# Keeping the residual stream transposed through both FFNs of a macaron block, with LayerNorm applied by GpSimd

## The chip, the core and the metric

The kernel runs on one core of one Trainium2 chip. The metric is device microseconds of one execution. A core has five engines with queues of their own: TensorE (PE), VectorE (DVE), ScalarE (ACT), GpSimd (POOL) and SyncE (SP), which here only issues DMAs.

## What is computed

A batch of 8 sequences of 1024 tokens with 128 features goes through FFN, attention and the same FFN again, in float32. Each stage is preceded by a LayerNorm without weights.

```python
x = x + 0.5 * ffn(layernorm(x))
x = x + attn(layernorm(x))
x = x + 0.5 * ffn(layernorm(x))

def ffn(x):                                    # T = 8192 tokens, D = 128
    scores = sigmoid(x @ gate_w.T)             # 16 experts
    _, idx = top_k(scores + gate_b, 4)
    w = scores[idx] / sum(scores[idx]) * 2.5   # comb: (T, 16), 4 entries a token
    for e in range(16):                        # all experts, INTER = 64
        gate, up = split(x @ w13[e].T)
        y += comb[:, e] * ((silu(gate) * up) @ w2[e].T)
    gate, up = split(x @ w13_s.T)
    return y + (silu(gate) * up) @ w2_s.T
```

## The kernel before

The 8192 tokens are 16 tiles of 512. `X` in SBUF holds the whole residual stream with tokens on the partitions. All matmuls of the FFN want features on the partitions, so a tile is transposed on the way in and its result on the way back. One 512-column product is three matmuls of split operands (`mm3`: high by high, high by low, low by high; `_h` and `_l` in the names), all of which stand in line L1318.

A tile T of an FFN is nine units j = 0 to 8 (eight pairs of experts and the shared expert). For each unit PE makes the gate and the up product (3 + 3 matmuls of 512 columns), ACT applies silu to the gate (L586), DVE multiplies by the routing weights (`ffn_weighted`, L933) and by up (`ffn_h`, L943), ACT rounds the result to `h_h` (`ffn_h_hi`, L551), POOL subtracts to get `h_l` (`low_half`, L412), and PE adds the down product three units later (LAG = 3), so that the downs of units 6 to 8 of a tile stand in units 0 to 2 of the next one. The two banks of gate, of up and of Y are used in turn.

Around these units lie, per tile:

- LayerNorm of tile T+2: DVE takes the statistics (`ffn_stats`, `ffn_mv`, `ffn_var`), POOL makes `rstd` and `neg_shift` (L416 to L421), ACT applies them to four blocks of 128 tokens (`ffn_xn`, L558).
- PE turns `xn` of tile T+1 with four 128x128 transposes at the start of the tile (`ffn_xnT`, L1402). ACT copies the bank to `xh`, DVE subtracts to get `xl` (L837).
- PE makes the router's logits of tile T+1 in unit 1; DVE works out the routing weights `comb` in some ten small instructions; PE turns `comb` in unit 5 (`ffn_combT`, L1416), ACT copies it, SP writes it to DRAM (L336) and reads it back broadcast over 64 partitions a row into `comb_b`, the memory of `qkT` (L341, ten DMAs).
- ACT copies the finished Y of tile T-1 to `yT`, PE turns it with four transposes in unit 4 (`ffn_y`, L1423), DVE adds it to `X` (`residual`, L987). In the second FFN SP then stores the tile.

Eight transposes a tile are thus of the residual stream. The loops over tiles take two tiles an iteration on every engine. Attention runs over 8 sequences in 8 steps each; its prologue is woven into the last two tiles of the first FFN, and the opening of the second FFN (`ffn_prep`) into the last sequence.

The order on each engine is written by hand and fixed; engines meet only through semaphores that count up. The edit touches these waits, among others:

```python
def ffn_combT(T):
    pe.wait_ge(route_step, ROUTE * (T + 1))
def ffn_down(T, q, j):
    pe.wait_ge(h_lo_done, UNITS * T + j + 1)
```

Of the kernel before, what the change touches and what calls it, by code (L numbers as in the profile page):

```python
# [14 lines left out]
P = 128  # L15
B, M, D = 8, 1024, 128
INTER, NEXP, TOPK = 64, 16, 4
ROUTE_SCALE = 2.5
EPS = 1e-5
# [11 lines left out]
PT_CHUNKS = 12  # L31

# [10 lines left out]
END_BANK = 4, 7  # L43
# [44 lines left out]
def macaron(nc, x, w13T, w2T, wqkvT, gwT, gate_b, ident_d, mask_d, cos_d, sin_d, comb_d, out):  # L88
    x_v = x.rearrange("b (n p) d -> p (b n) d", p=P)
    out_v = out.rearrange("b (n p) d -> p (b n) d", p=P)  # L90

    with ExitStack() as ctx:
# [9 lines left out]
        X = sb("X", [P, (B + 1) * QB, D])  # L102
        ident = sb("ident", [P, P])
# [48 lines left out]
        combT = [sb(f"combT{q}", [NEXP * NB, P]) for q in range(2)]  # L152
# [10 lines left out]
        v = [stage[:, v_at + p * M:v_at + (p + 1) * M].rearrange("p (n d) -> p n d", d=D) for p in range(2)]  # L163
        rope_c = [sb(f"rope_c{p}", [P, TILE]) for p in range(ROPE_BUFS)]
# [18 lines left out]
        yT = probT[0][:, NB:2 * NB, :].rearrange("p a c -> p (a c)")  # L183
# [13 lines left out]
        x_loaded = [sem(f"x_loaded{n}") for n in range(3)]  # L197
# [25 lines left out]
        neg_shift_done = sem("neg_shift_done")  # L223
        xn_done = sem("xn_done")
# [10 lines left out]
        comb_loaded = [sem(f"comb_loaded{n}") for n in range(len(COMB_PAIRS))]  # L235
# [8 lines left out]
        yT_done = sem("yT_done")  # L244
        yT_half = sem("yT_half")
        y_ready = sem("y_ready")
        y_half = sem("y_half")
        x_done = sem("x_done")
        stored = sem("stored")
# [41 lines left out]
        def end_blocks(a):  # L291

            at = NB * (TILES - 1) + NB // 2 * a
            return slice(at, at + NB // 2)
# [8 lines left out]
        def ln_count(T):  # L303

            return T + 1

# [4 lines left out]
        def _(sp):  # L311
# [10 lines left out]
            load(X[:, NB:2 * NB, :], x_v[:, NB:2 * NB, :], x_loaded[1])  # L322
            load(w13_f[:, early[2], :], w13T[:, early[2], :], w13_loaded[2])
            load(w2_f, w2T, w2_loaded)
            load(X[:, 2 * NB:3 * NB, :], x_v[:, 2 * NB:3 * NB, :], x_loaded[2])
# [5 lines left out]
            def comb_rows(T, q, first=0):  # L331
# [6 lines left out]
                src = comb_d[q].rearrange("(j a) t -> a j t", a=2)  # L338
                for g, (j0, j1) in enumerate(COMB_PAIRS):
                    for a in range(2 if j0 >= first else 0):  # L340
                        sp.dma_start(comb_b[q][a * INTER:(a + 1) * INTER, j0:j1, :],  # L341
                                     src[a:a + 1, j0:j1, :].to_broadcast([INTER, j1 - j0, TILE])
                                     ).then_inc(comb_loaded[g], 16)

            def store(t):
                sp.wait_ge(x_done, TILES + 1 + t)
                sp.dma_start(out_v[:, tile_blocks(t), :], X[:, tile_blocks(t), :]).then_inc(stored, 16)

            def ffn(base, stores):
                comb_rows(base, 0, 0 if stores else SPREAD)  # L350
                if stores:
                    sp.wait_ge(scores_ready, B * QB)
                else:
                    load(wqkv_f, wqkvT, attn_loaded)
                    load(mask[:], mask_d, attn_loaded)
                    load_x(3, 1)
                comb_rows(base + 1, 1)
                if not stores:
                    load_x(4, 0)
                    load(cos[:], cos_d, rope_loaded)  # L360
                    load(sin[:], sin_d, rope_loaded)
                with sp.Fori(0, TILES // 2 - (1 if stores else 3)) as k:
                    for q in range(2):
                        comb_rows(base + 2 * k + 2 + q, q)
                        if stores:
                            store(2 * k + q)
                        else:
# [1395 lines left out]
```

## Time and profile before

| | before |
|---|---|
| median of 3 runs | 861.89 us (861.54 to 862.0) |
| the profiled execution, its time | 863.0 us |
| its span | 861.2 us |
| granted TensorE clock | 0.998 |
| PE busy | 844.4 us, 98% |
| DVE busy | 694.2 us, 81% |
| ACT busy | 591.2 us, 69% |
| POOL busy | 557.6 us, 65% |
| DMA queue q1 | 88.58 MB, 41.3% of 16 engines |

The two FFNs take the stretches from 0 to about 340 us and from about 541 us to the end, attention the stretch between them. Busy shares are means over these. Ends of matmuls are modelled, so a busy PE is not a PE at its peak: the distance between the starts of two matmuls tells what one costs.

### The profile page before, as it was taken

How to read it: one execution, taken by the hardware profiler on the slowest of the kernel's cores; microseconds unless marked ns; L12 is line 12 of the kernel's file. 1: busy time of each engine (PE TensorE's matmuls, PEld its weight loads, DVE VectorE, ACT ScalarE, POOL GpSimd, SP SyncE). 2: the span in 40 equal slices, each digit the busy share in tenths (PEclk: the TensorE clock that was granted, in tenths of full speed). 3: DMA queues.
4: the chain of work that ended last, by engine and by line, in shares of the span. 5: the costliest groups of instructions: out<-in, count | busy, mean ns of one | idle time of the engine just before them, and what ended most of it. 6: DMA issues, size and time to landing. Idle time of an engine off the chain costs nothing.

```text
span 861.2 us, 18145 instructions
## 1 busy us (share of the span) xinstructions
PE 844.4 (98%) x4506; PEld 709.0 (82%) x4506; DVE 694.2 (81%) x2125; ACT 591.2 (69%) x1215; POOL 557.6 (65%) x519
## 2 busy tenths in 40 slices
PE   8999999999999999999999999999999999999998
PEld 7788888888888876889999998788888888888886
DVE  6888888888888887777776667788888888888885
ACT  5566666666666687777778866766666666666664
POOL 6666666666666678866767762466666666666664
PEclk9999999999999999999999999999999999999999
DMA  3684444455555341222111220445545444444553
GB/s 123 185 233 113 111 111 113 114 126 131 133 122 136 101 114 36 50 51 46 38 40 25 48 49 1 111 124 129 134 124 136 111 111 111 112 112 125 127 134 82
DMA packets 63494, 89.01 MB, mean 103 GB/s; under 512 B 7520, under 2 KB 26208, under 8 KB 63200
## 3 DMA queue, kind: packets, MB, share of 16 engines
q1 hardware_dynamic: 63456, 88.58, 41.3%
q8 instruction: 14, 0.23, 0.1%
q14 instruction: 24, 0.20, 0.1%
HBM read 74.92 MB, written 5.24 MB: 93 GB/s over the span
## 4 chain that ended last, share of the span: by engine, by line
PE 52%; ACT 4%; issue 2%; DVE 2%; POOL 1%; ACTq 0%; DVEq 0%; POOLq 0%
PE bank L1318 47%; PE bank L1628 3%; PE bank L1402 1%; PE bank L1423 1%; ACT prob L740 1%; ACT probT L551 1%; ACT xn L612 1%; ACT qkT L551 1%; ACT xh L551 0%; ACT xn L558 0%; POOL qkT L412 0%; DVE prob L933 0%; DVE X L1214 0%; DVE probT L943 0%; PE bank L1416 0%
## 5 line engine op out<-in xcount | busy, mean ns | idle before, releaser
L412 POOL TENSOR_TENSOR h_l<-probT,h_h 128x512 fp32r<-128x512 f32 x254 | 328.9, 1296 | 202.8 <-ACT h_h L551 202.7
L551 ACT ACTIVATE h_h<-probT 128x512 fp32r<-128x512 f32 (+1 forms) x286 | 179.5, 628 | 72.6 <-DVE probT L943 70.0
L1318 PE MATMUL bank<-xh,w_h 128*128 128x512 f32 x544 | 223.4, 411 | 2.0 <-DVE prob L933 1.9
L586 ACT ACTIVATE bank<-bank 128x512 f32<-128x512 f32 x252 | 146.2, 580 | 103.0 <-PE bank L1318 98.6
L1318 PE MATMUL bank<-xh,w_l 128*128 128x512 f32 x544 | 214.9, 395 | 0.0
L933 DVE TENSOR_TENSOR prob<-bank,qkT 128x512 f32<-128x512 f32 x252 | 173.5, 689 | 50.6 <-ACT bank L586 37.7
L1318 PE MATMUL bank<-xl,w_h 128*128 128x512 f32 x544 | 213.2, 392 | 0.0
L943 DVE TENSOR_TENSOR probT<-prob,bank 128x512 f32<-128x512 f32 x255 | 173.8, 681 | 12.7 <-DVE biased L874 5.0
L1318 PEld LDWEIGHTS bank<-xh,w_h 128*128 128x128 f32 x544 | 102.7, 189 | 23.9 <-DVE prob L933 2.7
L1318 PEld LDWEIGHTS bank<-xh,w_l 128*128 128x128 f32 x544 | 102.5, 188 | 23.9
L1318 PEld LDWEIGHTS bank<-xl,w_h 128*128 128x128 f32 x544 | 102.9, 189 | 19.5
L1318 PE MATMUL bank<-h_h,w_h 128*128 128x512 f32 x288 | 117.7, 409 | 1.0 <-POOL h_l L412 1.0
L1318 PE MATMUL bank<-h_h,w_l 128*128 128x512 f32 x288 | 114.3, 397 | 0.2 <-ACT h_h L551 0.2
L1318 PE MATMUL bank<-h_l,w_h 128*128 128x512 f32 x256 | 101.6, 397 | 0.0
L551 ACT ACTIVATE probT<-bank 128x512 f32<-128x512 f32 (+2 forms) x129 | 63.8, 510 | 39.5 <-PE bank L1628 37.8
L1318 PE MATMUL bank<-stage,probT 128*128 128x128 f32 x576 | 76.8, 279 | 4.4 <-DVE X L1214 2.0
L1318 PEld LDWEIGHTS bank<-stage,probT 128*128 128x128 f32 x576 | 71.1, 192 | 10.0 <-issue 4.7
L558 ACT ACTIVATE xn<-X,neg_shift,rstd 128x128 f32 (+1 forms) x128 | 61.2, 485 | 9.3 <-POOL neg_shift L421 9.3
L1318 PE MATMUL bank<-qkT 128*128 128x512 f32 (+3 forms) x288 | 66.5, 358 | 0.5 <-POOL qkT L412 0.5
L1318 PEld LDWEIGHTS bank<-h_h,w_h 128*128 128x128 f32 x288 | 54.3, 189 | 15.2 <-POOL h_l L412 2.1
L1318 PEld LDWEIGHTS bank<-h_h,w_l 128*128 128x128 f32 x288 | 54.5, 189 | 11.4 <-ACT h_h L551 0.6
L502 POOL TENSOR_TENSOR rope_s<-stage,sin 128x512 f32<-128x512 f32 x32 | 41.1, 1284 | 27.0 <-DMA stage<-stage 24.8
(117 smaller groups left out, 1332.4 us busy)
## 6 DMA issues: line engine op xcount, KB each, us to landing
qkT<-comb_rows SPq DMA_DIRECT2D x190, 256.0 KB, 5.2
qkT<-comb_rows SPq DMA_DIRECT2D x124, 128.0 KB, 2.9
stage<-stage SPq DMA_DIRECT2D x64, 128.0 KB, 2.4
X<-in_x SPq DMA_DIRECT2D x16, 256.0 KB, 6.2
out_x<-X SPq DMA_DIRECT2D x15, 256.0 KB, 5.8
comb_rows<-combT SPq DMA_DIRECT2D x32, 32.0 KB, 1.8
cos<-in_cos SPq DMA_DIRECT2D x1, 1024.0 KB, 8.3
sin<-in_sin SPq DMA_DIRECT2D x1, 1024.0 KB, 10.7
```

Of the source, the lines that this page charges most:

```text
L412: nc.gpsimd.tensor_tensor(lo, f, hi.bitcast(F32), ALU.subtract).then_inc(done, 1)
L502: nc.gpsimd.tensor_tensor(rope_s[s][:], qk_x[s], sin[:, w, t], ALU.mult).then_inc(rope_s_done, 1)
L551: return nc.scalar.activation(dst, src, ACT.Copy)
L558: ins = nc.scalar.activation(xn[:, n, :], X[:, bass.ds(NB * Tx + n, 1), :].rearrange("p a d -> p (a d)"), ACT.Identity, bias=neg_shift[:, ...
L586: nc.scalar.activation(bank[:, G_BANK[g], :], bank[:, G_BANK[g], :], ACT.Silu).then_inc(silu_done, 1)
L612: ins = nc.scalar.activation(xn[:, n, :], xb, ACT.Identity, bias=shift[:, n:n + 1], scale=root[:, n:n + 1])
L740: nc.scalar.activation(prob[s][:, 0:w], bank[:, 2 * s:2 * s + 2, :].rearrange("p a c -> p (a c)")[:, 0:w], ACT.Exp, bias=negmax[s][:], sca ...
L933: nc.vector.tensor_tensor(weighted[j % 2], bank[:, G_BANK[(q + j) % 2], :], comb_b[q][:, j, :], ALU.mult).then_inc(weighted_done, 1)
L943: nc.vector.tensor_tensor(h_place(T, q, j), weighted[j % 2], bank[:, u, :], ALU.mult).then_inc(h_done, 1)
L1318: return nc.tensor.matmul(dst, lhsT, rhs, start=start, stop=stop)
L1402: ins = nc.tensor.transpose(bank[:, T_BANK, n * P:(n + 1) * P], xn[:, n, :], ident[:])
L1628: ins = nc.tensor.transpose(bank[:, probT_bank(i, c, last), a * P:(a + 1) * P], prob[s][:, k0:k0 + P], ident[:])
```

## The change

The FFNs keep the residual stream of a tile with features on the partitions, in a ring `xT` of four buffers of 512 columns (in the free part of `stage`), beside `X`.

- First FFN: x is loaded a second time, from an array that the host has transposed (`load_xT`, 256 KB a tile). The residual is added to `xT` straight from the Y bank (`residual`). PE turns the result with four transposes (`ffn_y`, now in unit 6), ACT copies them to `X` for attention (`ffn_X`).
- Second FFN: PE turns `X` of tile T+2 at the start of tile T (`ffn_xT`), ACT copies the bank to `xT`; the residual is added there, and the tile is stored to a transposed output, which the host turns back. The last tile is done in two halves.
- LayerNorm from tile 2 of each FFN on: POOL writes -mean and rstd of tile T+3 into two more columns a block of `comb` (`ffn_rows`), which travel with the routing weights through `ffn_combT` and DRAM. SP reads the two rows back, broadcast to all partitions (`rows`, one DMA of 512 KB a tile). POOL computes `xc = xT + rows[0]`, `xs = xc * rows[1]` and, after ACT has copied `xs` to `xh`, `xl = xs - xh`.
- Gone are the four ACT instructions of `ffn_xn`, DVE's `ffn_xl`, the copy `ffn_yT` and PE's `ffn_xnT` for these tiles. Tiles 0 and 1 of each FFN take the former way.
- Statistics of X are taken a tile earlier (T+3 in tile T). All loops take four tiles an iteration, and PE's code of the second FFN is written out tile by tile but for its attention part.

```diff
@@ SP
+            def load_xT(T, r):
+                sp.wait_ge(y_ready, T - RING + 1)
+                sp.dma_start(xT[r], x_t[:, bass.ds(TILE * T, TILE)]).then_inc(xT_moved[r], 16)
...
+                if ahead:
+                    wait(sp, xs_done, scaled_count(T + 1, base))
+                    sp.dma_start(rows[:], comb_d[q, NEXP:NEXP + 2, :].rearrange("(a e) t -> a e t", a=1
+                                                                                ).to_broadcast([P, 2, TILE])
+                                 ).then_inc(rows_loaded, 16)
...
+                        store(4 * k + TILES + c, c)
+                        comb_rows(4 * k + TILES + 2 + c, c % 2, 0, TILES)
@@ POOL
+            def ffn_rows(T, q):
+                pool.wait_ge(var_done, ln_count(T))
+                wait(pool, combT_ready, T - 2)
+                nc.gpsimd.tensor_tensor(comb[:, NEXP + 1, :], var_eps[:, at], neg_half[:, at], ALU.pow).then_inc(rstd_done, 1)
+                nc.gpsimd.tensor_tensor(comb[:, NEXP, :], mv[:, at, 0], neg_one[:, at], ALU.mult).then_inc(neg_mean_done, 1)
+            def ffn_center(T, base, turn, c):
+                n = scaled_count(T, base)
+                pool.wait_ge(rows_loaded, 16 * n)
...
+                nc.gpsimd.tensor_tensor(xc, xT[c], rows[:, 0, :], ALU.add).then_inc(xc_done, 1)
+            def ffn_scale(T, base):
...
+                nc.gpsimd.tensor_tensor(xs, xc, rows[:, 1, :], ALU.mult).then_inc(xs_done, 1)
+            def ffn_xl(T, q):
+                pool.wait_ge(xh_done, T + 1)
+                low_half(xl[q][:], xs, xh[q][:], xl_done)
...
+                    if j == PAIRS - 1 and ahead:
+                        ffn_xl(T + 2, q)
                     pool.wait_ge(h_hi_done, UNITS * T + j + 1)
...
-                    elif j == 2 and not last:
-                        ffn_rstd(T + 2)
+                    elif j == 2 and (t is None or t + 3 < TILES):
+                        ffn_rows(T + 3, 1 - q)
+                    if j == 3 and ahead:
+                        ffn_center(T + 2, base, turn + (c + 2) // RING, (c + 2) % RING)
+                    elif j == 5 and ahead:
+                        ffn_scale(T + 2, base)
@@ ACT
+            def ffn_xh(T, q, base):
+                act.wait_ge(gate_ready, UNITS * (T - 1))
+                act.wait_ge(xs_done, scaled_count(T, base))
+                copy(xh[q][:], xs).then_inc(xh_done, 1)
...
-                    if j == 0 and not last and not start:
-                        ffn_xh(T + 1, 1 - q)
...
+                    if j == UNITS - 1 and ahead:
+                        ffn_xh(T + 2, q, base)
...
-                    if j == LAG and not first:
-                        ffn_yT(T - 1, 1 - q)
...
-                    elif 0 <= at < NB and not last:
-                        ffn_xn(T + 2, Tx + 2, at)
@@ DVE
+            def residual(T, c, parts=1):
+                dve.wait_ge(down_done, UNITS * (T + 1))
...
+                    nc.vector.scalar_tensor_tensor(xT[c][:, cols], bank[:, Y_BANK[c % 2], cols], 0.5, xT[c][:, cols],
+                                                   ALU.mult, ALU.add).then_inc(xr_done, 1)
...
-                ffn_xl(N, 1 - q)
...
+                    if j == NB and not first:
+                        residual(T - 1, back)
...
@@ DVE, opening
                 ln_apply(NB, 0, xn_done)
+                dve.wait_ge(x_loaded[1], 16)
+                ffn_stats(1, 1, 1)
+                ffn_stats_wait(1)
+                ffn_mv(1, 1)
+                ffn_var(1, 1)
                 ffn_xl(0, 0)
-                dve.wait_ge(x_loaded[1], 16)
-                for n in range(NB):
-                    ffn_stats(1, 1, n)
-                ffn_stats_wait(1)
+                dve.wait_ge(x_loaded[2], 16)
+                ffn_stats(2, 2, 0)
+                ffn_stats_wait(2)
@@ PE
-            def ffn_combT(T):
+            def ffn_combT(T, ahead=True):
                 pe.wait_ge(route_step, ROUTE * (T + 1))
+                if ahead:
+                    pe.wait_ge(rstd_done, ln_count(T + 2))
+                    pe.wait_ge(neg_mean_done, ln_count(T + 2))
...
-            def ffn_tile(T, q, first, last, first_batch=None):
-                if not last:
+                if first:
                     ffn_xnT(T + 1)
+                if base and (t is None or t + 2 < TILES):
+                    ffn_xT(T + 2, T + 2 - base)
...
-                    if j == 4 and not first:
+                    if base:
+                        if first and j in (2, 4):
+                            ffn_xT(T + j // 2 - 1, j // 2 - 1)
+                    elif j == 6 and not first:
...
-                        ffn_y(T - 1)
+                        ffn_y(T - 1, (c - 1) % RING)
```

How the order moves on the engines. First PE, at the head of the tile loop of the first FFN, before: the branch row opens the loop, L1402 is the transposes of `xn`, then come the gate and the up product of unit 0 and a down product.

```order
L1489 UNCONDITIONAL_BRANCH
L1489 ISA
L285 REGISTER_ALU [waits xn_done]
L1402 MATMUL bank<-ident,xn 128x128 [waits combT_done]
L1402 MATMUL bank<-ident,xn 128x128 x3
L285 ISA
L1318 MATMUL bank<-xh,w_h 128x512 [waits weighted_done]
L1318 MATMUL bank<-xl,w_h 128x512
L1318 MATMUL bank<-xh,w_l 128x512
```

The same place of the changed kernel:

```order
L1632 UNCONDITIONAL_BRANCH
L1632 ISA
L1438 MATMUL bank<-xh,w_h 128x512 [waits weighted_done]
L1438 MATMUL bank<-xl,w_h 128x512
L1438 MATMUL bank<-xh,w_l 128x512
```

The tile now begins with its gate product. Next PE again, from unit 4 on, before: the four transposes of `yT` stand ahead of unit 5.

```order
L1318 MATMUL bank<-h_l,w_h 128x512
L1423 MATMUL bank<-ident,probT 128x128 [waits x_done,yT_done]
L1423 MATMUL bank<-ident,probT 128x128 x3
L1434 REGISTER_ALU
L1318 MATMUL bank<-xh,w_h 128x512 [waits weighted_done]
```

In the changed kernel they read `xT` (the memory of `stage`) and stand behind the down product of unit 6:

```order
L1438 MATMUL bank<-h_l,w_h 128x512
L1547 MATMUL bank<-ident,stage 128x128 [waits x_done,xr_done]
L1547 MATMUL bank<-ident,stage 128x128 x3
L1566 REGISTER_ALU
L1438 MATMUL bank<-xh,w_h 128x512 [waits weighted_done]
```

Last POOL, one tile from behind unit 2 on, before: the three small LayerNorm instructions and then one subtraction a unit.

```order
L415 REGISTER_ALU
L416 TENSOR_TENSOR rstd<-var_eps,neg_half 128x4 [waits var_done]
L418 TENSOR_TENSOR neg_mean<-mv,neg_one 128x4
L421 TENSOR_TENSOR neg_shift<-neg_mean,rstd 128x4 [waits rstd_done,neg_mean_done]
L439 REGISTER_ALU
L412 TENSOR_TENSOR h_l<-probT,h_h 128x512 [waits h_hi_done]
```

The same stretch of the changed kernel, up to the `xl` of the tile after next:

```order
L453 TENSOR_TENSOR h_l<-probT,h_h 128x512 [waits h_hi_done]
L475 REGISTER_ALU
L479 ISA [waits rows_loaded]
L483 TENSOR_TENSOR xn<-stage,rows 128x512 [waits xs_done,xT_moved3]
L520 REGISTER_ALU
L453 TENSOR_TENSOR h_l<-probT,h_h 128x512 [waits h_hi_done]
L520 REGISTER_ALU
L453 TENSOR_TENSOR h_l<-probT,h_h 128x512 [waits h_hi_done]
L489 REGISTER_ALU [waits xc_done]
L490 TENSOR_TENSOR xn<-xn,rows 128x512 [waits xl_done]
L520 REGISTER_ALU
L453 TENSOR_TENSOR h_l<-probT,h_h 128x512 [waits h_hi_done]
```

Two instructions of 512 columns stand between the subtractions of units 3 to 6 (their output `xn` is the memory of `xc` and `xs`), and a third, `xl`, follows ahead of that of unit 7.

## Rows read from the trace of the kernel before

**Rows 1.** The page, part 1: busy time, share of the span, instructions.
```profile
PE 844.4 (98%) x4506; PEld 709.0 (82%) x4506; DVE 694.2 (81%) x2125; ACT 591.2 (69%) x1215; POOL 557.6 (65%) x519
```

**Rows 2.** Chain that ended last, second FFN: start us, us, what ran.
```profile
599.09 0.44 PE bank L1402 x4
599.53 11.10 PE bank L1318 x52
...
618.83 0.44 PE bank L1402 x4
```

**Rows 3.** Timeline of PE, first FFN: start us, us, engine, line, what, count.
```profile
153.28 0.40 PE L1318 MATMUL bank<-h_l,w_h 128*128 128x512 f32 x1
153.51 0.60 PE L1402 MATMUL bank<-ident,xn 128*128 128x128 f32 x4
153.88 0.48 PE L1318 MATMUL bank<-xh,w_h 128*128 128x512 f32 x1
154.19 0.39 PE L1318 MATMUL bank<-xl,w_h 128*128 128x512 f32 x1
...
155.35 0.40 PE L1318 MATMUL bank<-h_h,w_h 128*128 128x512 f32 x1
...
156.75 0.18 PE L1318 MATMUL bank<-gw_hl,xh 128*128 128x32 f32 x1
```

**Rows 4.** Groups by line: busy us, mean ns | idle before, who ended it.
```profile
L412 POOL TENSOR_TENSOR h_l<-probT,h_h 128x512 fp32r<-128x512 f32 x254 | 328.9, 1296 | 202.8 <-ACT h_h L551 202.7
...
L416 POOL TENSOR_TENSOR rstd<-var_eps,neg_half 128x4 f32<-128x4 f32 x33 | 33.3, 1008 | 12.4 <-DVE var_eps L982 12.3
...
L1402 PE MATMUL bank<-ident,xn 128*128 128x128 f32 x128 | 19.3, 274 | 1.9 <-DVE xn L831 1.3 <-ACT combT L551 0.5
...
L1423 PE MATMUL bank<-ident,probT 128*128 128x128 f32 x124 | 18.6, 272 | 0.0
```

**Rows 5.** Windows: us, busy PE, PEld, DVE, ACT, POOL; clock, DMA share, GB/s.
```profile
153.00:173.00 20.00, 20.00 (x96) 16.41 (x96) 17.17 (x52) 13.52 (x27) 13.20 (x13) 1.00 0.52 123
```

**Rows 6.** Timeline of POOL, the same tile as rows 3: units 3 and 6.
```profile
166.07 1.30 POOL L412 TENSOR_TENSOR h_l<-probT,h_h 128x512 fp32r<-128x512 f32 x1
...
171.86 1.31 POOL L412 TENSOR_TENSOR h_l<-probT,h_h 128x512 fp32r<-128x512 f32 x1 [0.73 <-ACT h_h L551]
```

**Rows 7.** Timeline of PE, last tile of the first FFN, bracket: idle before.
```profile
333.70 0.50 PE L1318 MATMUL bank<-h_h,w_h 128*128 128x512 f32 x1 [0.69 <-POOL h_l L412]
```

**Rows 8.** Timelines of DVE and POOL: the variance instruction, beside POOL's subtraction and alone.
```profile
157.97 0.17 DVE L982 TENSOR_SCALAR var_eps<-mv 128x4 f32<-128x4 f32 x1
...
518.55 0.82 DVE L982 TENSOR_SCALAR var_eps<-mv 128x4 f32<-128x4 f32 x1
...
518.06 1.28 POOL L412 TENSOR_TENSOR qkT<-rot,qkT 128x512 fp32r<-128x512 f32 x1 [1.03 <-ACT qkT L551]
```

**Rows 9.** A window of one us, second FFN, columns as in rows 5.
```profile
588.00:589.00 1.00, 1.00 (x6) 0.81 (x5) 0.83 (x6) 0.67 (x3) 0.09 (x1) 1.00 0.09 25
```

**Rows 10.** Timeline of SP, the same tile: DMA issues.
```profile
574.70 0.48 SPq L336 DMA_DIRECT2D comb_rows<-combT  x1
576.54 6.28 SPq L341 DMA_DIRECT2D qkT<-comb_rows  x10
```

**Rows 11.** Timelines of DVE and POOL, opening of the first FFN.
```profile
7.50 2.53 POOL L412 TENSOR_TENSOR w_l<-stage,w_h 128x512 fp32r<-128x512 f32 x2 [0.78 <-DVE xn L831]
...
8.87 0.69 DVE L837 TENSOR_TENSOR xl<-bank,xh 128x512 fp32r<-128x512 f32 x1 [1.44 <-ACT xh L551]
9.47 0.86 DVE L968 BATCH_NORM_STATS2 stats<-X 128x6 f32<-128x128 f32 x4
```

**Rows 12.** Timeline of PE's weight loads, opening of the second FFN.
```profile
543.32 0.19 PEld L1318 LDWEIGHTS bank<-gw_hl,xh 128*128 128x128 f32 x1 [1.15 <-DVE xl L837]
```

**Rows 13.** Chain that ended last, the end of the kernel.
```profile
856.99 0.39 ACT probT L551
...
857.97 0.42 DVE X L963
```

More of the change, by code:

```diff
@@ L622, in comb_spread, with ffn_tile @@
                                                            ).to_broadcast([P, NB, 2, INTER])).then_inc(spread_copied, 1)
-            def ffn_tile(T, Tx, q, first, last, first_batch=None, start=False):
+            def ffn_tile(base, turn, c, first_batch=None):
+                T, q = RING * turn + c, c % 2
+                first, last, t = False, False, None
+                if isinstance(T, int):
+                    t = T - base
+                    first, last = t == 0, t == TILES - 1
+                start = first and base == 0
+                ahead = t is None or t + 2 < TILES
                 for j in range(UNITS):
@@ L630, in ffn_tile @@
                             attn_hi(FIRST_HI[j], 0, 0)
-                    if j == 0 and not last and not start:
-                        ffn_xh(T + 1, 1 - q)
+                    if j == 0 and first and not start:
+                        opening_xh(T + 1, 1 - q)
                     if j == (7 if start else 6) and not last:
@@ L642, in ffn_tile @@
                         ffn_gsilu(T + 1)
-                    if j == LAG and not first:
-                        ffn_yT(T - 1, 1 - q)
+                    if base:
+                        if j == 0 and ahead:
+                            ffn_xT(T + 2, turn + (c + 2) // RING, (c + 2) % RING)
+                        elif first and j in (3, 5):
+                            ffn_xT(T + (j - 3) // 2, turn, (j - 3) // 2)
+                    elif j == PAIRS - 1 and not first:
+                        ffn_X(T - 1, T - 1)
                     at = j - (UNITS - 1 - NB)
@@ L984, in residual @@
[L984 to L994 removed]
+                nc.vector.tensor_scalar_add(var_eps[:, at], mv[:, at, 1], EPS).then_inc(var_done, 1)
@@ L995, in ffn_tile @@
+            def ffn_tile(base, turn, c, first_batch=None):
+                T, q = RING * turn + c, c % 2
+                first, last, t = False, False, None
+                if isinstance(T, int):
+                    t = T - base
+                    first, last = t == 0, t == TILES - 1
+                start = first and base == 0
+                stats_next = t is None or t + 3 < TILES
+                N, L, Lx, back = T + 1, T + 3, T + 3 - base, (c - 1) % RING
                 if start:
```

450 lines of the change are left out of this document (247 added, 203 removed).

## The prediction

> **What bounds the kernel now.** I read the page first: PE is busy for 98% of the span, the others for 81% at most [rows 1]. A busy PE may still be one that is served late, so I went to the chain that ended last. In the FFNs it consists of PE alone: 11.10 us of matmuls, 0.44 us of four transposes, more matmuls, and the same transposes again after 618.83 - 599.09 = 19.74 us [rows 2]. This period repeats through both FFNs. In a window of 20 us DVE is busy for 17.17, ACT for 13.52, POOL for 13.20, and the clock is full [rows 5]. So the period is PE's own work, and whatever leaves PE's queue shortens it, as long as no other engine gets into the way. POOL always waits for ACT's `h_h` (202.7 us in all [rows 4]); it has room, but it also ends each unit's chain, which goes gate, silu, `weighted`, `h`, `h_h`, `h_l`, down product.
>
> **What a block of four transposes costs PE.** Matmuls of 512 columns start 0.23 us apart. The block starts 0.23 us behind its forerunner, the next matmul 0.37 us behind the block, and the one after it 0.31 instead of 0.23 us later [rows 3]. So a block costs 0.37 + 0.08 = 0.45 us; the chain says 0.44. I take 0.445.
>
> **How many go.** L1402 has 128 and L1423 124 transposes [rows 4], and the end of the kernel (`ffn_end`) has four more: 64 blocks. Afterwards there are 18 in each FFN: in the first two of `xn` and sixteen of `xT`, in the second two of `xn` and sixteen of `X`. That is 28 fewer, 28 x 0.445 = 12.5 us. The ones in the first FFN all come from tiles 1 to 14. In the second, its first tile gets three more (`ffn_xT` of its tiles 2, 0 and 1) and the rest seventeen fewer. That first tile waits for others: in front of the router's logits PE stood for 1.15 us until DVE had `xl` [rows 12], and the block of `ffn_xT` now stands just there. Between none and all three blocks (1.3 us) can be hidden; I take two, 0.9 us more gain.
>
> **The end.** The last Y goes through ACT's copy at 856.99, transposes and DVE's sum at 857.97 [rows 13]. DVE now reads Y directly, so its first half starts where ACT did: 1.0 us less. Both ways end with two stores.
>
> **The opening of the first FFN.** DVE's order changes: the statistics of tile 1 come ahead of `xl` of tile 0. That `xl` ran at 8.87 and the statistics behind it at 9.47 [rows 11]. Now 0.86 us of statistics and the variance precede it. The variance instruction has a trap: alone it takes 0.17 us, but beside a POOL subtraction that began at 518.06 and ended at 519.34 it took from 518.55 to 519.37 [rows 8]; it waits until POOL's instruction is over. Here POOL splits weights from 7.50 to 10.03 [rows 11], so the variance ends near 10.2 and `xl` starts about 1.3 us late. PE's first logits hang on it, and the statistics of tile 2, behind which the router's chain stands, add some 0.2 us. I take +1.5; the lower bound is 0 (all hidden), the upper +3, should X of tile 2 land late.
>
> The Trainium skill has this rule ("SBUF — State Buffer", section "Who interferes with whom"): DVE in a two-port mode and GpSimd share a pair of ports as an exclusive lock, held for the whole instruction. The trace agrees (0.82 beside 0.17 us). Without the lock the first term would be 0.9 instead of 1.3.
>
> **The preparation of the second FFN.** The last sequence of attention gets the statistics of one more tile on DVE, 0.86 us and two small instructions, between softmax maxima. DVE has holes there. From 0 to +0.8; I take +0.3.
>
> **What moves to POOL.** A tile now costs nine subtractions at 1.29, pow and mult at 1.01 + 0.20, and `xc`, `xs`, `xl`. The last three are of the same shape, so 1.29 each, 3.9 us. Sum 16.7 us of a period of 19.74 - 0.45 = 19.29, 87%. It fits, but the order matters. Walked along rows 6: the subtraction of unit 3 ends at 166.07 + 1.30 = 167.37; `xc`, units 4 and 5, `xs` and unit 6 follow nearly without a gap, at 1.25 to 1.29 each, and end at 173.4 to 173.8 instead of 173.17. PE wants unit 6 at its down product, before at 155.35 + 19.74 = 175.09 [rows 3, 6], now 0.9 us earlier in the first FFN, 174.2. What were 1.9 us of slack are 0.4 to 0.8. `xl` of the tile after next waits for ACT's `xh`, which waits for the last gate product of this tile. It ends about 21.3 us after the tile's start, and the logits (before 156.75 - 153.51 = 3.24 us into the next tile, now 2.8) want it at 22.1: 0.8 us. The subtraction of unit 7 waits behind `xl`, and down product 7 behind it, with about 1 us. All of it fits by less than one POOL instruction.
>
> Others gain room. ACT loses four `xn` and gets nothing longer, so nothing is late for it but `h_h` of unit 7, by one copy of 0.6 us, counted above. DVE loses `xl` (0.69) and the residual moves from unit 7 to unit 4, right behind the routing chain, where DVE has no holes: units 5 and 6 come about 0.6 us later, with about that much to spare. Since slacks of 0.4 us won't hold in every tile, I book 0.05 us of waits for each of 26 tiles: +1.3.
>
> **DMA.** Per tile 512 KB of `rows` come, and 256 KB of `xT` in the first FFN. Ten broadcast loads (2 MB) and a store are issued from 576.54 on [rows 10]; in the window from 588 the engines are nearly idle (share 0.09 [rows 9]), and the next write is due at 574.70 + 19.74 = 594.4 [rows 10]. So 2.25 MB took some 11 us, 0.75 MB more take 3.7, and over 6 us are free. `rows` are ready some 2 to 3 us before POOL asks. In the second FFN the store of tile T-1 now stands in SP's queue ahead of the write of `comb` and waits for the residual. Both become due about together, so the routing weights come later by 0 to 1.2 us (256 KB at the same rate). The free time says that DVE doesn't live from hand to mouth here, and it never waited for such a load. Cost nothing, bounded by 0 and 0.5 us a tile.
>
> **Sum.** -12.5 - 0.9 - 1.0 + 1.5 + 0.3 + 1.3 = -11.3 us. The profiled execution took 863.0 us, 1.1 above the median of 861.89. Against its own time that gives 851.7, as a median 850.6.
>
> **Rivals.**
> - *POOL's slack is used up (0.22).* If walking along the rows was 0.5 us too kind, PE waits in each of 26 tiles, for `h_l` of unit 6 or for `xl`. For it speaks the last tile of the first FFN: with rope's instructions between subtractions PE stood 0.69 us for `h_l` [rows 7]. Against it, POOL has 2.6 us a tile left. At 0.3 instead of 0.05 us a tile: 850.6 + 6.5 = 857. The Trainium skill advises VectorE, not GpSimd, for elementwise work ("GPSIMD Engine Reference", section "Engine selection"); the trace's 1.29 beside 0.69 us agrees.
> - *Slower: the lock between DVE and POOL (0.08).* POOL is now busy when DVE's variance instruction comes, in each tile. It can wait for up to 1.29 us [rows 8], and behind it stands the routing chain, then `comb`, then PE's `ffn_combT`. Should this reach PE, the price is about 0.65 us a tile, 27 x 0.65 = 17.5, hence 868. It decides from 0.42 us a tile on. Against it: DVE loses `xl` in front of this very place and then waits for the logits anyway.
> - *Routing weights late in the second FFN (0.06).* The store in front and `rows` behind; at 0.5 us for 15 tiles 858.
> - *Something in the new loops, or a wait that I misread (0.02).*
>
> **How the numbers follow.** The forecast case has 0.62; its own range is 848.5 to 853.5 (start from 0 to 3, first tile of the second FFN from 0 to 1.3, waits from 0 to 0.1 a tile). 8 in 10 reach over most of the first rival: 848 to 858. 0.2% (1.7 us) is about what a measurement can tell from no change. Faster: 0.62 + 0.21 + 0.04 = 0.87; same 0.03; slower 0.10.
>
> **What would show it.** PE's period in both FFNs 19.3 us, without idle time ahead of down products, logits or `comb`'s transpose. 144 transposes of these kinds. POOL at about 77% of the span (557.6 + 27 x 3.7 = 657 us), waiting before units 0 to 2 only. First logits near 11.0. The last sum about 1 us earlier against the last matmul. The prediction is wrong if the period stays above 19.45, and the wait that stands there tells which rival it is.

## The result, and the profile after

| | before | after |
|---|---|---|
| median (lowest to highest) | 861.71 us (861.41 to 862.0) | 871.26 us (868.4 to 875.1) |
| profiled execution, its span | 863.0, 861.2 us | 875.1, 873.3 us |
| granted clock, mean | 0.998 | 0.987 |

The change made the kernel slower: the ratio after to before is 1.0109, with an interval of 1.0093 to 1.0126. I had forecast 850.6 us. Four runs of the changed kernel lie 6.7 us apart, those of before 0.6 us. Medians in this document are over all executions of a kernel; ratios and intervals leave out four single executions of 912 to 2455 us (two of before, one each of e7 and e9).

The page of the kernel after, part 1, against [rows 1]:

```profile
PE 844.1 (97%) x4394; PEld 700.1 (80%) x4394; DVE 680.9 (78%) x2088; ACT 548.8 (63%) x1098; POOL 654.4 (75%) x572
```

PE has 112 instructions less, and 28 blocks of four transposes are indeed gone, as these groups by line show (DVE, ACT and POOL moved as forecast too). Yet PE is busy for as long as before.

```profile
L1555 PE MATMUL bank<-ident,X 128*128 128x128 f32 x64 | 9.6, 272 | 0.0
L1547 PE MATMUL bank<-ident,stage 128*128 128x128 f32 x64 | 9.6, 272 | 0.0
...
L1522 PE MATMUL bank<-ident,xn 128*128 128x128 f32 x16 | 2.5, 276 | 2.3 <-ACT combT L637 1.2 <-DVE xn L932 1.1
```

To find where time went, I took a mark that each tile leaves once, SP's write of `comb`, and subtracted neighbours. The timeline of SP of the kernel after, second FFN:

```profile
605.11 0.34 SPq L362 DMA_DIRECT2D comb_rows<-combT  x1
...
624.52 0.33 SPq L362 DMA_DIRECT2D comb_rows<-combT  x1
...
643.97 0.33 SPq L362 DMA_DIRECT2D comb_rows<-combT  x1
...
666.58 0.34 SPq L362 DMA_DIRECT2D comb_rows<-combT  x1
...
686.31 0.34 SPq L362 DMA_DIRECT2D comb_rows<-combT  x1
```

A steady tile of the second FFN takes 19.41 to 19.46 us (in the first up to 19.50, before 19.74), but this one 22.61. There are four such tiles, two in each FFN (23.79, 23.96, 22.61, 23.68 us). DVE's timeline in the long one, then PE's first instruction behind its gap, then windows of all engines (columns as in [rows 5]):

```profile
649.30 0.69 DVE L1045 TENSOR_TENSOR probT<-prob,bank 64x512 f32<-64x512 f32 x1 [1.75 <-POOL h_l L453]
653.59 0.87 DVE L1060 BATCH_NORM_STATS2 stats<-X 128x6 f32 x4 [3.59 <-issue]
```

```profile
655.46 0.50 PE L1438 MATMUL bank<-xh,w_h 128*128 128x512 f32 x1 [1.91 <-DVE prob L1032]
```

```profile
652.00:655.00 3.00, 1.54 (x7) 0.93 (x6) 1.16 (x5) 0.00 (x0) 1.10 (x1) 1.00 1.02 236
...
656.00:657.00 1.00, 1.00 (x4) 0.58 (x3) 1.00 (x4) 0.63 (x2) 0.00 (x0) 0.76 1.14 252
657.00:658.00 1.00, 1.00 (x3) 0.74 (x3) 0.96 (x4) 0.49 (x2) 0.92 (x1) 0.50 1.02 244
658.00:659.00 1.00, 1.00 (x4) 0.77 (x3) 1.00 (x3) 0.74 (x2) 0.40 (x2) 0.50 0.96 223
...
660.00:661.00 1.00, 1.00 (x6) 0.79 (x6) 0.97 (x6) 1.00 (x2) 0.25 (x1) 1.00 0.06 25
```

DVE stands still for 3.59 us and the profile finds nothing that it waited for ("issue"). In the second FFN these statistics read `X` that has long been in SBUF, so it is no load. PE runs dry, and then the granted clock falls from 1.00 to 0.50 (from 2.4 to 1.2 GHz) and stays there for about three microseconds. At the four jumps of this profile PE stood for 1.9 to 3.0 us, and the reduced clock lasted 3 to 3.5 us in three cases and over 6 in the fourth. PE is "busy" with slow matmuls, which hides the loss in its busy time. DVE's waits over the whole kernel (us in total, times, longest):

```profile
DVE stats L1060 <- issue: 17.3, 4, 4.7
...
DVE prob L1032 <- DVE stats L1060: 5.3, 23, 0.3
DVE prob L1032 <- DVE take L990: 5.2, 24, 0.5
...
DVE probT L1042 <- DVE biased L975: 4.2, 22, 0.2
```

All four stand at `ffn_stats` (L1060) of the first tile of a turn, where DVE jumps back to the start of its loop. The diff changed these loops from two tiles a turn to four. By the program's own count, which leaves out the instructions that only wait for a semaphore, that is some 173 and 336 instructions of DVE; with every instruction that the trace records, registers and semaphores too, it is 214 rows from one jump to the next before and 419 after. DVE's next row, one that sets registers, stands 0.25 us behind a jump before, and 3.9 to 5.0 us behind it after. The loop at L1277 is entered once in each FFN and makes three turns, hence two jumps back in each.

What the engine stands for can be seen too. The instruction queues are rows of their own in the DMA view, and in the window of the gap, 650.0 to 653.3, there is this:

```profile
q14 instruction: 1, 0.01, 0.6%
```

The packet starts at 651.47, 2.0 us behind the jump, and DVE goes on 1.9 us behind its start. This and the experiments' profiles hold 34 gaps at a jump back. In each of them a packet of q14 starts, and DVE goes on 1.9 to 2.6 us behind that start. The profile doesn't say which engine a packet is for, but a gap that never comes without one, and ends so evenly behind it, is the mark of a fetch.

### The profile page after: what moved, and what is told of

Same layout as the page of the kernel before. It is cut to its first block, busy times and chain, and to the rows that moved or that the text cites. A ratio compares the mean times of both kernels' runs of the same rounds, so it can differ in the third digit from the quotient of the medians.

```text
span 873.3 us, 17406 instructions
## 1 busy us (share of the span) xinstructions
PE 844.1 (97%) x4394; PEld 700.1 (80%) x4394; DVE 680.9 (78%) x2088; ACT 548.8 (63%) x1098; POOL 654.4 (75%) x572
## 4 chain that ended last, share of the span: by engine, by line
PE 30%; POOL 12%; issue 10%; ACT 4%; DVE 2%; POOLq 0%; DVEq 0%; ACTq 0%
PE bank L1438 27%; POOL h_l L453 6%; PE bank L1766 2%; POOL xl L453 1%; POOL h_h L453 1%; POOL xn L483 1%; POOL comb L469 1%; POOL xn L490 1%; ACT prob L841 1%; ACT xn L711 1%; ACT probT L637 1%; ACT qkT L637 1%; DVE stats L1060 0%; ACT xh L637 0%; ACT xn L645 0%
## 5 line engine op out<-in xcount | busy, mean ns | idle before, releaser
L1438 PE MATMUL bank<-xh,w_l 128*128 128x512 f32 x544 | 217.2, 399 | 0.0
L1032 DVE TENSOR_TENSOR prob<-bank,qkT 128x512 f32<-128x512 f32 x252 | 171.6, 681 | 28.2 <-ACT bank L690 16.6
L637 ACT ACTIVATE probT<-bank 128x512 f32<-128x512 f32 (+2 forms) x96 | 45.1, 490 | 38.7 <-PE bank L1766 38.4
L453 POOL TENSOR_TENSOR qkT<-rot,qkT 128x512 fp32r<-128x512 f32 x32 | 41.0, 1283 | 25.3 <-ACT qkT L637 25.3
```

The lines of the kernel that those rows point to most:

```text
L453: nc.gpsimd.tensor_tensor(lo, f, hi.bitcast(F32), ALU.subtract).then_inc(done, 1)
L637: return nc.scalar.activation(dst, src, ACT.Copy)
L1032: nc.vector.tensor_tensor(weighted[j % 2], bank[:, G_BANK[(q + j) % 2], :], comb_b[q][:, j, :], ALU.mult).then_inc(weighted_done, 1)
L1438: return nc.tensor.matmul(dst, lhsT, rhs, start=start, stop=stop)
```

## The experiments

**1. VectorE straight, and the counter-test.** These four share a question: is it the jump on DVE, and is the rest of the change innocent?

```diff
 # e1_dve_straight: changed kernel, DVE block
-                with dve.Fori(0, TURNS - 1) as k:
+                for k in range(TURNS - 1):
 # e2_before_dve4: kernel before, DVE block
-                with dve.Fori(0, TILES // 2 - (2 if start else 1)) as k:
-                    for q in (1, 0):
+                with dve.Fori(0, 3) as k:
+                    for a in range(2):
+                        for q in (1, 0):
...
 # (e2 also writes out the two tiles of the second FFN that are left over)
 # e3_others_straight: as e1, but in the blocks of PE, ACT and POOL
 # e4_all_straight: in all four
```

> The changed kernel with VectorE's code of both FFNs written out straight instead of as a loop of three turns of four tiles; no instruction is changed. Theory A (the jump back to the start of VectorE's loop, now four tiles long, starves VectorE of instructions for 3.6 to 4.7 us, four times in the kernel, and the tensor engine idles and loses its clock behind it): the tiles that now last 22.6 to 24.0 us fall to about 19.4, which gives back about 16.8 us, so 854 to 856 us, and no stall of VectorE that waits for nothing. Rival B (POOL's two new passes and the port that it shares with VectorE hold the chain up): stays at 871 +- 1. Rival C (the new loads of rows and of x saturate the DMA queues around those points): stays at 871, the stalls of VectorE stand where they stood. Rival D (the longer loops of PE, ACT or POOL are late, and VectorE only shows it): stays at 871.

> The kernel before, with VectorE's loop of both FFNs taking four tiles a turn instead of two (three turns in each FFN, and two more tiles written out in the second); no instruction is changed, and none of the change's transposes, loads or POOL passes is there. Theory A: a stall of about 3.6 to 4.7 us before the second and third turn of each FFN, four in all, so 861.7 + 4 x (3.5 to 4.5) = 876 to 880 us. Rivals B and C: 861.7 +- 1, since POOL and the queues are as before. Rival D (other engines' loops): 861.7 +- 1.

> The changed kernel with the FFN loops of PE (first FFN), ACT and POOL written out straight, and VectorE's kept as a loop of four tiles. Theory A: VectorE's four stalls stay, 869 to 872 us, at most 1 to 2 us less if the tensor engine's short waits for nothing in the first FFN (4.8 us in 11 pieces) go with its loop. Rival D (their loops are the cause): 854 to 856 us. Rivals B and C: 871 +- 1.

> The changed kernel with the FFN loops of PE, ACT, POOL and VectorE all written out straight. Theory A: like the kernel with VectorE's alone written out, 854 to 856 us, less at most 1 us for the other engines. Rival D: more than 3 us below the kernel with VectorE's alone written out. If straight code costs a fetch of its own, it is above it.

| | median, us | ratio to before, interval |
|---|---|---|
| e1, DVE straight | 850.01 (849.67 to 850.85) | 0.9857 (0.9842 to 0.9872) |
| e2, before with DVE loops of four tiles | 876.34 (874.46 to 880.69) | 1.0166 (1.0143 to 1.0189) |
| e3, the others straight | 869.51 (866.57 to 871.11) | 1.0073 (1.0055 to 1.0091) |
| e4, all straight | 849.50 (848.48 to 849.60) | 0.9848 (0.9833 to 0.9863) |

Theory A holds in both directions: taking DVE's jumps away gives 21.3 us back, and putting them into the kernel before, which has nothing else of the change, costs 14.5 us (3.6 for each jump; in the changed kernel it is more, as the account below shows). B, C and D each expected no difference in e1 and in e2, and D 854 to 856 us in e3. The sizes were half missed: e1 and e4 lie 4 to 6 us below the 854 to 856 that I expected, since I had counted the long tiles alone and not the 0.14 us of every other tile, the tiles behind the long ones and the opening. Part 1 of the page of e1, and its SP timeline:

```profile
PE 831.7 (98%) x4394; PEld 697.5 (82%) x4394; DVE 686.7 (81%) x2088; ACT 549.5 (65%) x1098; POOL 655.1 (77%) x572
```

```profile
666.75 0.34 SPq L362 DMA_DIRECT2D comb_rows<-combT  x1
...
686.07 0.33 SPq L362 DMA_DIRECT2D comb_rows<-combT  x1
```

The tile is 19.32 here, 19.29 on average. In e2 the same four gaps are there, now at `ffn_xl` (L837), the first DVE instruction of a turn in that kernel. Its waits and its timeline:

```profile
DVE xl L837 <- issue: 15.0, 4, 4.1
```

```profile
114.31 0.69 DVE L946 TENSOR_TENSOR probT<-prob,bank 64x512 f32<-64x512 f32 x1 [0.21 <-ACT prob L589]
119.09 0.69 DVE L837 TENSOR_TENSOR xl<-bank,xh 128x512 fp32r<-128x512 f32 x1 [4.09 <-issue]
```

**2. What kind of stall it is.** A hint to the instruction fetch, another place in instruction memory, and the control that the 11.8 us are not straight code's own.

```diff
 # e5_dve_hint
-                with dve.Fori(0, TURNS - 1) as k:
+                with nc.Fori(0, TURNS - 1, engines=bass.OrderedEngineSet([dve.engine]), hint_back_edge=True) as k:
 # e6_dve_slot0: the same with head_slot={dve.engine: 0} in place of the hint
 # e7_before_straight: kernel before, DVE block
-                with dve.Fori(0, TILES // 2 - (2 if start else 1)) as k:
+                for k in range(TILES // 2 - (2 if start else 1)):
 # e9_half_the_jumps
-                with dve.Fori(0, TURNS - 1) as k:
+                with dve.Fori(0, TURNS - 2) as k:
...
+                for c in range(1, RING + 1):
+                    ffn_tile(base, TURNS - 2 + turn + c // RING, c % RING)
```

> The changed kernel with VectorE's FFN loops kept at three turns of four tiles, and the branch at their end announced to the engine's instruction fetch by a prefetch hint at the start of each turn; all else is the changed kernel. Theory A (the jump back has to wait until the instructions at the loop's start, no longer held by the engine, are fetched from memory): the four stalls of 3.6 to 4.7 us shrink to under 0.5 us and the time falls to that of the kernel with VectorE's code straight, 850 to 852 us. If the stall were a cost of taking a branch at all, or of the counters at the loop's end, it would stay, 869 to 872 us.

> The changed kernel with each of VectorE's FFN loops (some 336 instructions a turn) placed so that its first instruction opens a block of 256 in instruction memory. Theory A with the loop's length as the cause: the stalls stay, 868 to 873 us, since a turn still spans two blocks. Theory A with the place as the cause (the turn spans three blocks only by where it happens to start): the stalls go, 850 to 852 us.

> The kernel before with VectorE's code of both FFNs written out straight; none of the change is in it. This tells whether part of the 11.8 us that the changed kernel gains with straight code belongs to straight code itself. The trace of before shows no stall of VectorE at the end of its two-tile loops, so 861.8 +- 1 us; 855 or less would say that the gain was the loop's and not the transposes'.

> The changed kernel with VectorE's FFN loops cut to two turns of four tiles, the third written out behind them: one jump back in each FFN in place of two. Theory A: two stalls in place of four, so the changed kernel's time less half of the 21.3 us that straight code gives back, 860 to 861 us, and the tiles behind the first jump last 22 to 24 us, those where the second was 19.4. If the size of the loop were to cost something in each tile and not at the jump, the time would fall by a third of it, to 864 us.

e5 measured 859.73 us (856.59 to 863.04; ratio 0.9960, 0.9944 to 0.9977), e6 870.12 (866.07 to 871.91), e7 862.95 beside 862.48 of before (ratio 1.0009, 0.9999 to 1.0019), e9 860.93 (ratio 0.9975, 0.9961 to 0.9989). So straight code alone gains nothing in before, the price goes with the number of jumps (two fewer gave 10.3 of the 21.3 us; about 1 of the 10.3 is the loop form of the eight tiles that e9 writes out, see part 4), and shifting the loop doesn't help.

The hint was half a miss: all tiles of the loops took 19.4 to 19.6 us, no stall at a jump was left, but two new ones came. DVE's waits, and its timeline at the first of them:

```profile
DVE probT L1042 <- issue: 4.1, 1, 4.1
...
DVE prob L1032 <- issue: 2.2, 1, 2.2
```

```profile
280.14 0.22 DVE L975 TENSOR_TENSOR biased<-bank,gb 128x64 f32<-128x64 f32 x1
284.46 0.69 DVE L1042 TENSOR_TENSOR probT<-prob,bank 128x512 f32<-128x512 f32 x1 [4.10 <-issue]
```

This is in the tile behind the loop's end, the other one at 817.66 in the same tile of the second FFN: with the jump announced, it is now the way straight on that isn't ready. Both gaps hold one packet of q14 again, and they come in straight code, so what these gaps share with the others is the fetch and not the jump. Busy DMA engines don't make such a gap: before's loops jump back at a DMA share of 0.66 to 0.91 without one. They seem to lengthen it. From the jump to DVE's next row, the 7 gaps with a share below 0.83 have a median of 3.3 us, the 18 with 0.97 and more one of 4.8; but e5's gap of 4.1 us came at 0.52. The queue q14 of part 3 of the page (packets, MB) tells the same. The first row is of the kernel after, the second of e1, the third of e5:

```profile
q14 instruction: 51, 0.42, 0.2%
```

```profile
q14 instruction: 38, 0.31, 0.1%
```

```profile
q14 instruction: 31, 0.25, 0.1%
```

The loop, with far less code, fetched more than straight code (51 to 38 packets), and the packets in the gaps say why: it fetched its own start again. The queue serves more engines than DVE, so the numbers are to be read as differences. In the kernel before, going to loops of four tiles took the same queue from 24 packets to 48.

The Trainium skill has this rule ("Runtime: NRT & Kernel Launch", section "Instruction fetch mechanics"): an engine holds two blocks of 256 instructions, fetched in sequence, and a taken branch to a place outside them waits for a fetch. The runs agree in kind: turns of 173 (before) and 189 (attention) instructions show no such wait, turns of 336 one of 2.6 to 5.5 us each. Counted with semaphore instructions these are 214, 224 and 419. That 419 is less than two blocks didn't save it, even with the start on a block's first place (e6). Where between 224 and 419 it begins was not measured. It also differs by engine: PE's turns in the first FFN of the changed kernel hold 361 matmuls and as many weight loads, and its next weight load stands 0.02 us behind the jump.

**3. POOL's slack.**

```diff
 # e8_pool_more: e1, and in ffn_center (ffn_scale then also waits for extra_done)
+                nc.gpsimd.tensor_tensor(xs, xT[c], rows[:, 0, :], ALU.add).then_inc(extra_done, 1)
                 nc.gpsimd.tensor_tensor(xc, xT[c], rows[:, 0, :], ALU.add).then_inc(xc_done, 1)
 # e10_scale_later (all loops kept), e11_straight_scale_later (all straight): POOL's ffn_tile
-                    if j == PAIRS - 1 and ahead:
+                    if j == PAIRS and ahead:
                         ffn_xl(T + 2, q)
+                        pool.wait_ge(xl_done, T + 3)
...
-                    elif j == 5 and ahead:
+                    elif j == 6 and ahead:
                         ffn_scale(T + 2, base)
 # e12_straight_rope_later: e11, and e16_straight_rope_later: e4, with
-FIRST_SIN, FIRST_ADD = {2: 0, 4: 1}, {3: 0, 5: 1}
+FIRST_SIN, FIRST_ADD = {3: 0, 5: 1}, {4: 0, 6: 1}
```

> The changed kernel with VectorE's code straight, and one more POOL pass over 512 columns in each tile (28 in all, of 1.29 us, with a result that is overwritten): the suspected cost of the change on POOL made half as large again. If POOL has slack of that size in each tile (it is busy some 16 of 19.3 us): 850 to 852 us. If POOL's slack is used up, as the rival of the prediction had it: up to 28 x 1.3 = 36 us more, 860 to 886 us. If the two engines' shared port costs VectorE about 1 us in each tile: PE's period goes from 19.29 to above 19.4.

> The changed kernel, all loops kept, with two of POOL's passes one unit later: the scaling pass (xs) behind the low half of unit 6, and the low half of x (xl) behind that of unit 7. Theory A for the 0.14 us by which a steady tile is longer with all loops (19.43 against 19.29): VectorE waits 1.8 us for POOL's low half of unit 6, since the scaling pass stands ahead of it, and has no idle time from there to the routing weights, for which PE then waits 0.4 us. With the pass later VectorE starts 1.25 us earlier, and the steady tile falls to 19.29; the four stalls stay: 866 to 869 us. Rival: the low half of x now comes so late that PE waits for it before the routing's product: the tile is 19.5 or more, 872 or above.

> All engines' FFN code straight, and POOL's two passes one unit later. PE has no idle time left in a steady tile at 19.29, so the steady tile stays; what can be gained is in the tiles at the ends of the FFNs: 848.5 to 850 us, against 849.5 with straight code alone.

> As the one before, and POOL's two sine products of the first attention batch one unit later in the last tile of the first FFN (units 3 and 5 instead of 2 and 4, their additions at 4 and 6). There POOL waited 2.2 us for the DMA that swaps the halves (4.3 us in the profile of the kernel with VectorE straight), and the low halves of h queue behind it, for which PE waited 1.5 us: 847 to 849 us. If the additions are then late for PE, 849 to 851 us.

e8: 865.69 us (861.8 to 868.59). Its SP timeline gives a tile of 19.87 to 19.89 us:

```profile
718.34 0.33 SPq L363 DMA_DIRECT2D comb_rows<-combT  x1
738.21 0.34 SPq L363 DMA_DIRECT2D comb_rows<-combT  x1
```

1.29 us more of POOL's time cost 0.58 us a tile, so about 0.7 us of slack was left. I had expected 850 to 852 us if POOL had slack of that size, and up to 886 if it had none: the truth lies between. e10, e11 and e12 were bad misses: 945.28, 939.73 and 938.70 us (ratios 1.097, 1.090 and 1.0896). PE's timeline in e11 and windows around it (busy PE, clock, DMA share, GB/s):

```profile
699.87 0.28 PE L1439 MATMUL bank<-gw_hl,xh 128*128 128x32 f32 x1 [1.75 <-POOL xl L453]
```

```profile
698.00:700.00 2.00, 0.25 (x3) 1.00 1.06 248
...
702.00:705.00 3.00, 3.00 (x9) 0.53 0.89 241
```

`xl` now came after a wait for unit 7's `h_h` and one more subtraction, and PE stood before each tile's logits (58.1 us in 28 times in e10). In e11 these waits are 56.8 of the 90.2 us that it lies above e4. Its mean granted clock is 0.963 against 0.999, and 0.036 of its 939.5 us are 34 us, which is the rest: 2.0 us of waiting and 1.2 us of lost clock a tile. A late `xl` stood as the rival in e10's expectation, priced much too low, and in those of e11 and e12 not at all. POOL's own wait for `xl_done`, which came with the move, was not tested apart.

**4. The last 0.14 us a tile.** The steady tile (second FFN) is 19.43 with all loops kept, 19.29 with DVE's written out and 19.28 with all the others'.

```diff
 # e13_act_straight: changed kernel, only ACT's FFN loop written out; e14_pool_straight: only POOL's
 # e15_pool_less: changed kernel, in ffn_center, and ffn_scale then reads xT[c] instead of xc,
 #   so that x is scaled without its mean taken off
-                nc.gpsimd.tensor_tensor(xc, xT[c], rows[:, 0, :], ALU.add).then_inc(xc_done, 1)
+                nc.gpsimd.tensor_tensor(xc[:, 0:1], xT[c][:, 0:1], rows[:, 0, 0:1], ALU.add).then_inc(xc_done, 1)
```

> The changed kernel with ScalarE's FFN loops alone written out straight. If it is ScalarE's loop form (waits against a register's value in each step) that makes the routing chain 0.14 us late in each tile, the steady tile is 19.29; else 19.43. The four stalls stay in both cases: 867 to 872 us.

> The changed kernel with POOL's FFN loops alone written out straight. If it is POOL's loop form, the steady tile is 19.29, else 19.43. The four stalls stay: 867 to 872 us.

> The changed kernel, all loops kept, with POOL's centering pass cut to one column (x is scaled without its mean taken off, so the routing is another; all other instructions stand), 28 x 1.25 us of POOL's time less. If VectorE is late for the routing weights because POOL's low half of unit 6 comes late, it comes 1.25 us earlier, and the steady tile falls from 19.43 to 19.29 us, with the four stalls as they are: 866 to 869 us. If POOL is not in that chain: 19.43 us and 869 to 872.

> All engines' FFN code straight, POOL's passes as in the change, and POOL's two sine products of the first attention batch one unit later (units 3 and 5). 849.5 us without the move; POOL's wait of 2.2 us for the swapped halves is then over before POOL comes to it, but PE waited for nothing behind it in that profile: 848 to 849.5 us.

e13 measured 871.18 us with tiles of 19.36 to 19.39 in the second FFN, e14 870.54 with 19.33 to 19.36, e15 874.32 with 19.43 to 19.46 (two executions each). So it is not POOL's extra pass, and neither engine alone: ACT's loop form adds 0.06 us and POOL's 0.08, DVE's 0.14 (e3 has DVE's loop and 19.28, so once the others are quick there is room for it). A likely place, though not shown by a run of its own, is in DVE's waits for itself. In the waits of the kernel after that are shown above, DVE waits some 0.2 us three times a tile for its own last result; in e1, where DVE waits against constants instead of the loop's register, the profile shows none of them (four tiles are 280 rows there in place of 419; the 151 that only set registers are gone). PE meets the sum at `comb`'s transpose (PEld waited 3.6 us for `comb` in ten tiles after, 0.8 us in three in e1). How much each instruction form costs was not measured by itself. e16 measured 849.43 us (848.21 to 851.72), the same as e4, so POOL's wait for the swapped halves wasn't worth anything.

The best version is the changed kernel with all FFN loops written out (849.5), or just DVE's (850.0): 12.3 and 11.8 us below before.

## Why the prediction was wrong

The step that failed is the one that isn't in the sum: the change also doubled the loops' bodies, and I priced that at nothing. It appears only as the last rival, "Something in the new loops, or a wait that I misread (0.02)", without place or price. I took the loops' form for free because before had loops and no stall at their ends; but that row said only that 173 instructions are free. What the runs showed in its place: a stall of 3.6 to 4.7 us of DVE at each of four jumps back, and a loop form that costs 0.14 us a tile once the order is tight. The price was 21.3 us against a gain of 11.8: 850.0 + 21.3 = 871.3.

Where the 21.3 lie, from tile marks: the four tiles with a jump are 3.2 to 4.5 us above their neighbours (16.3 in all) and those behind them another 0.2 to 1.5 (2.4); the opening was 2.4 us later than in e1 at the third mark; 0.14 us in each of some 21 other tiles are 2.9. That is 24.0, for two profiled spans that differ by 873.3 - 849.1 = 24.2 us; the medians differ by less, since gaps and opening vary from run to run. The 2.4 us of the opening don't come with the loop: the first mark lies at 18.77 in e1 and 20.41 after, but at 18.75 in e13, which keeps DVE's loop, and at 20.43 in e11, which is all straight. What sets it was not looked for.

With the jumps away, the terms can be read one by one in e1. Each is read from one profile, so a difference of a few tenths of a microsecond may be that execution's own:

- *Transposes.* The period is 19.29, as forecast (19.74 - 0.445).
- *The first tile of the second FFN, two of three blocks hidden.* PE waits 0.28 us ahead of the logits behind one block; before, it waited 0.71 there. (The 1.15 of [rows 12] is the idle time of the weight load, which is 0.7 in e1.) Both fell by one block, and from the first transpose of `xn` to the logits it is 2.01 us in both kernels: the block ahead is hidden. From these logits to the fifth mark e1 is 1.10 us shorter than before, where three tiles at 0.445 would make it 1.34; so all three blocks together cost 0.24 us, and rather 2.5 than two were hidden.

```profile
539.26 0.28 PE L1438 MATMUL bank<-gw_hl,xh 128*128 128x32 f32 x1 [0.28 <-DVE xl L938]
```

- *The end, 1.0 us.* The last matmul ended at 845.9 (chain: 844.59 + 1.29) and DVE's sum began at once; before, the same distance was 1.0 us [rows 13].

```profile
845.91 0.76 DVE L1087 SCALAR_TENSOR_TENSOR stage<-bank,stage 128x256 f32<-128x256 f32 x2 [0.65 <-PE bank L1438]
```

- *The opening, +1.5.* The first logits came at 10.77 against 9.70, so +1.07. The trap is there and sets the time: the variance ended at 10.04, just behind POOL's split (10.01), where I had put 10.2. It took only 0.34 us because DVE came to it late, after 0.96 us for X of tile 1, a wait that I had not seen and that the trap hides. In the other profiles of changed kernels it took from 0.43 to 1.25 us and ended at 9.9 to 10.2, with the logits at 10.6 to 11.0. In e14 alone it started at 8.77, took 0.17 us, and the logits came at 9.81: it must have fallen between POOL's two subtractions (7.61 to 10.15), so 1 us of this term is a matter of luck.

```profile
9.70 0.34 DVE L1075 TENSOR_SCALAR var_eps<-mv 128x4 f32<-128x4 f32 x1
```

- *Preparation of the second FFN, +0.3.* Between the last mark of the first FFN and the first of the second lie 230.80 us in e1, 228.72 in e4, 229.21 before. The +1.6 of e1 lie in the last tile of the first FFN, where POOL waited 4.3 us for the swapped halves and PE then 1.5 for `h_l`. The statistics cost nothing visible.
- *Waits, 0.05 us in 26 tiles.* With DVE straight there are none in a steady tile. In the kernel after it was 0.14 us, from the code's form.
- *POOL.* 655.1 us busy against 657 forecast, slack 0.7 us against 0.4 to 0.8 walked. The first rival didn't come true, but was near: one more pass brings it about.
- *The lock.* It stands in each tile (variance 0.66 us in the steady tile after, 0.83 in e1) and costs nothing: the period is 19.29, as forecast without it, and PE's weight loads wait for `comb` 0.8 us in the whole of e1. DVE has 1.4 to 1.8 us a tile of waiting for `h_l` in which a delay can vanish; that this is the reason is likely, not shown.
- *DMA, 0.* `rows` and `xT` cost nothing; DVE's waits for routing weights sum to 2.7 us in e1.

As measured the sum is -12.5 - 1.1 - 1.0 + 1.1 + 1.6 + 0 = -11.9 us. The sum of -11.3 us was thus right within half a microsecond (e1: -11.8) and the prediction wrong by 20.7, for the length of the loops. That e1 meets 850.6 is partly luck: opening and waits were booked too high, the last tiles of the first FFN too low.

## What to carry to other kernels

Count the instructions of each engine in a loop's body before and after a change, and treat a body that grows well past what the trace shows to be free as a new cost: here one gap of about 4 us at each jump back, plus what the consumer loses. In the trace it is an idle time with "issue" as its cause, ahead of the first instruction of a turn, on one engine only, with a packet on an instruction queue inside it. "Issue" alone is not enough: in e11, whose DVE code is straight, DVE shows 30.7 us of it in 25 pieces ahead of the multiplication by the routing weights (L1033), and the piece that ends at 697.68 has no such packet in it. When PE is the bound, price a gap at more than its length, because the clock halved behind it here. And a walk along the rows that ends in slacks of 0.7 us says not only that an order fits, but that moving one pass in it can cost several times what the whole change was to gain (74 us in e10), while a move outside that walk (e16) cost nothing.

## What the runs showed of the hardware that I had not expected

A jump back over 336 instructions of VectorE (419 with those for semaphores) stalled it for 2.6 to 5.5 us, 34 times out of 34, each time with a packet of an instruction queue in the gap, 1.9 to 2.6 us ahead of its end; over 189 (224) it didn't. The gap tended to be longer where the DMA engines were fuller (medians 3.3 and 4.8 us), which no run varied on purpose. A prefetch hint removes the gap at the jumps (none at four) and one gap each appears behind the two loops' exits. TensorE jumped back over 361 matmuls and as many weight loads without a gap. A loop can fetch more instruction packets than the same code written out (51 against 38). Gaps of PE of 1.9 to 3.0 us were followed by 3 to over 6 us at reduced clock, mostly half (0.50), which a busy share of 97% hides.
